# Four output buffers and an uneven deal of the last blocks to three sums, in the expert stage of a gated cross-attention block

## What is computed

```python
topk_p, topk_i = jax.lax.top_k(probs, TOP_K)
topk_p = topk_p / jnp.sum(topk_p, axis=-1, keepdims=True)
gates = gates.at[jnp.arange(T)[:, None], topk_i].add(topk_p)
def r_body(acc, p):
    w1, b1, w2, b2, g = p
    return (acc + g[:, None] * (jnp.maximum(flat @ w1 + b1, 0.0) @ w2 + b2), None)
routed_out, _ = jax.lax.scan(r_body, jnp.zeros_like(flat), (rw1, rb1, rw2, rb2, gates.T))
...
x = x + jnp.tanh(g_ffn[0]) * (shared_out + routed_out)
```

## Time and profile before

| what | us |
|---|---|
| median of three runs | 386.02 |
| the three runs | 383.51 to 388.60 |
| the profiled execution | 387.09 |
| its span in the trace | 385.3 |
| expert stage, first to last scatter issued | 218.7 to 368.3 |
| busy in the whole span: PE, DVE, ACT, POOL | 333.4, 240.6, 214.6, 221.7 |

### The profile page before, as it was taken

How to read it: one execution, slowest core, us unless ns; L and a number is a source line. 1 busy time by engine, 2 the same in 40 slices (tenths; PEclk the granted TensorE clock), 3 DMA queues, 4 the chain that set the end, 5 groups by cost and what they waited for, 6 DMA issues and landing times.

```text
span 385.3 us, 8620 instructions
## 1 busy us (share of the span) xinstructions
PE 333.4 (87%) x2574; PEld 262.3 (68%) x2574; DVE 240.6 (62%) x753; ACT 214.6 (56%) x537; POOL 221.7 (58%) x267
## 2 busy tenths in 40 slices
PE   8889999999899988786772999999999999999800
PEld 5567766666666664564541898999999999999700
DVE  7997788789789888569310355555555545445426
ACT  4795899979878877232130455555555555555400
POOL 8466332103013456757774288888788888787830
PEclk9999999999999999699786899999999999999965
DMA  7799999996004014613233488888888888897688
GB/s 227 208 309 310 308 326 315 320 237 205 4 2 134 19 60 125 204 60 117 101 116 125 128 125 144 137 151 138 139 146 147 142 143 141 138 146 108 76 195 282
DMA packets 63295, 62.20 MB, mean 161 GB/s; under 512 B 6258, under 2 KB 61588, under 8 KB 63252
## 3 DMA queue, kind: packets, MB, share of 16 engines
q1 hardware_dynamic: 48532, 44.60, 40.5%
q0 software_dynamic: 13680, 17.05, 27.4%
q10 hardware_dynamic: 1040, 0.01, 0.2%
HBM read 29.01 MB, written 32.63 MB: 160 GB/s over the span
## 4 chain that ended last, share of the span: by engine, by line
PE 55%; DVE 12%; issue 10%; POOL 9%; DMA 8%; ACT 5%; SPq 0%; POOLq 0%; DVEq 0%
PE psum L1608 14%; PE psum L1590 10%; POOL rows_by_block L502 7%; PE psum L1301 6%; PE psum L1348 5%; DVE nmax L906 5%; DMA sum<-ob,xs 5%; PE psum L1581 4%; PE psum L1599 3%; ACT probs L625 2%; PE psum L1319 2%; PE psum L1196 2%; PE psum L1282 2%; PE psum L1401 2%; POOL sum L546 2%
## 5 line engine op out<-in xcount | busy, mean ns | idle before, releaser
L546 POOL DMA_INDIRECT sum<-ob,xs x79 | 122.4, 1549 | 40.1 <-DVE ob L1166 26.9
L906 DVE TENSOR_REDUCE nmax<-psum 128x2 f32<-128x512 f32 x128 | 80.9, 683 | 13.2 <-PE psum L1301 12.3
L1608 PE MATMUL psum<-w,hT 88*128 (+1 forms) x316 | 81.5, 380 | 0.0
L625 ACT ACTIVATE probs<-psum 128x512 f32<-128x512 f32 x128 | 69.5, 599 | 15.3 <-PE psum L1319 13.8
L1166 DVE TENSOR_SCALAR ob<-psum,gate 128x256 f32<-128x256 f32 x79 | 38.2, 484 | 53.5 <-PE psum L1608 38.1
L755 ACT ACTIVATE hT<-psum,b1b 88x128 f32<-88x128 f32 x158 | 48.8, 357 | 35.6 <-PE psum L1599 34.6
L1590 PE MATMUL psum<-w,xT 128*128 x316 | 61.6, 318 | 0.3 <-ACT xT L746 0.3
L1608 PEld LDWEIGHTS psum<-w,hT 88*128 88x128 f32 (+1 forms) x316 | 53.8, 190 | 4.6 <-issue 0.3
L746 ACT ACTIVATE xT<-psum 128x256 f32<-128x256 f32 x79 | 30.3, 384 | 46.3 <-PE psum L1581 46.2
L502 POOL DMA_INDIRECT rows_by_block<-Vx,slot x48 | 47.6, 991 | 14.4 <-issue 14.1
L425 POOL CAST Qx<-nmax 128x8 fp32r<-128x8 f32 x32 | 6.3, 197 | 74.2 <-DVE nmax L906 74.1
(11 more groups left out here) (194 smaller groups left out, 468.6 us busy)
## 6 DMA issues: line engine op xcount, KB each, us to landing
rows_by_block<-blank SPq DMA_DIRECT2D x1, 10744.0 KB, 38.2
xs<-rows_by_block SPq DMA_DIRECT2D x79, 136.0 KB, 2.9
w<-in_L_ffn_rw_dram SPq DMA_DIRECT2D x2, 2816.0 KB, 22.1
w<-in_L_ffn_rw_dram SPq DMA_DIRECT2D x16, 352.0 KB
sum<-blank SPq DMA_DIRECT2D x3, 1152.0 KB, 13.4
w<-sum SPq DMA_DIRECT2D x12, 256.0 KB, 5.3
sum<-ob,xs POOLq DMA_INDIRECT x79
x_sb<-in_x_dram SPq DMA_DIRECT2D x4, 256.0 KB, 3.9
```

The source lines that it names most:

```text
L546: pool.indirect_dma_start(yd[i], bass.IndirectOffsetOnAxis(ap=xs[b % ROWS_AHEAD][:, X_ID:X_ID + 1].bitcast(U32), axis=0), ob[i][:, :], Non ...
L625: act.activation(probs[g % 2][:, :, n, :], st_bank(g, n)[:, :].rearrange("p (t q) -> p t q", t=TB), ACT.Exp, scale=SCALE).then_inc(exp_ok, 1)
L906: dve.tensor_reduce(nmax[i % 2][:, :, n], S_BANK[(4 * i + n) % SB][:, :].rearrange("p (t k) -> p t k", t=TB), AX.X, ALU.max, negate=True). ...
L1608: ins = pe.matmul(Y_BANK[b % 2][:, 0:D], hT[b % 2][0:rows, c, :], w2[0:rows, bass.ds(expert[b], 1), c, :].rearrange("p a n -> p (a n)"), s ...
```

## The change

There are now four buffers `ob`, used as b mod 4, while there are still three sums. Which sum a block goes to stands in a list: b mod 3 for blocks 0 to 74, and then 0, 1, 0, 1 for blocks 75 to 78, so that sum 2 gets its last scatter from block 74. `added_before(b)` counts the earlier blocks of the same sum, and every wait on `summed` is worked out from it: DVE's wait ahead of writing a buffer is now for block b-4, POOL's for the last block of the same sum (b-3, but b-2 for blocks 77 and 78), SP's for block b-12 as before. The sums are read back and added in the order of their last blocks: 2, 0, 1. A spare piece of SBUF shrinks by the fourth buffer's size, so the later tensors keep their places.

```diff
-    SUMS, ROWS_AHEAD = 3, 12
-    SPARE = 1488
-    assert ROWS_AHEAD % SUMS == 0 and HC < P
+    SUMS, ROWS_AHEAD, OUTS = 3, 12, 4
+    SPARE = 1232
+    assert HC < P
+    sum_of = [b % SUMS for b in range(NB)]
+    sum_of[NB - 4:] = [(NB - 4) % SUMS, (NB - 3) % SUMS] * 2
+    order = sorted(range(SUMS), key=lambda i: max(b for b in range(NB) if sum_of[b] == i))
+    in_sum = [sum_of.count(i) for i in range(SUMS)]
+    def added_before(b):
+        return sum_of[:b].count(sum_of[b])
...
-        ob = [sb(f"ob{i}", [P, D]) for i in range(SUMS)]
+        ob = [sb(f"ob{i}", [P, D]) for i in range(OUTS)]
...
             for n in range(SUMS):
-                i = (NB + n) % SUMS
-                sp.wait_ge(summed[i], 16 * len(range(i, NB, SUMS)))
+                i = order[n]
+                sp.wait_ge(summed[i], 16 * in_sum[i])
...
             for b in range(NB):
-                i = b % SUMS
+                i = sum_of[b]
                 pool.wait_ge(ob_ok, b + 1)
-                if b >= SUMS:
-                    pool.wait_ge(summed[i], 16 * (b // SUMS))
+                if added_before(b):
+                    pool.wait_ge(summed[i], 16 * added_before(b))
                 pool.indirect_dma_start(yd[i], ...
-                                        ob[i][:, :], None, compute_op=ALU.add).then_inc(summed[i], 16)
+                                        ob[b % OUTS][:, :], None, compute_op=ALU.add).then_inc(summed[i], 16)
...
             def block_out(b):
-                i = b % SUMS
                 dve.wait_ge(o_mm, b + 1)
                 dve.wait_ge(gate_ok, b + 1)
-                if b >= SUMS:
-                    dve.wait_ge(summed[i], 16 * (b // SUMS))
-                dve.tensor_scalar(ob[i][:, :], Y_BANK[b % 2][:, 0:D], gate[b % 2][:, 0:1], None, ALU.mult).then_inc(ob_ok, 1)
+                if b >= OUTS:
+                    dve.wait_ge(summed[sum_of[b - OUTS]], 16 * (added_before(b - OUTS) + 1))
+                dve.tensor_scalar(ob[b % OUTS][:, :], Y_BANK[b % 2][:, 0:D], gate[b % 2][:, 0:1], None, ALU.mult).then_inc(ob_ok, 1)
```

More of the change, by code:

```diff
@@ L351, in _ @@
                     sp.wait_ge(xb_mm, b - ROWS_AHEAD + 1)
-                    sp.wait_ge(summed[b % SUMS], 16 * ((b - ROWS_AHEAD) // SUMS + 1))
+                    sp.wait_ge(summed[sum_of[b - ROWS_AHEAD]], 16 * (added_before(b - ROWS_AHEAD) + 1))
                 sp.dma_start(xs[r][:, :], xd[b * P:(b + 1) * P, :]).then_inc(xs_ld[r], 16)
             for n in range(SUMS):
-                i = (NB + n) % SUMS
-                sp.wait_ge(summed[i], 16 * len(range(i, NB, SUMS)))
+                i = order[n]
+                sp.wait_ge(summed[i], 16 * in_sum[i])
                 if n == 0:
```

## The result

The changed kernel is a little slower. Its median over 20 executions is 387.89 us against 385.52 us of the kernel before in the same comparison. The ratio is 1.0055, 95% interval 1.0031 to 1.0079; it isn't that of the two medians, since it leaves out executions more than 1.5% above the fastest of their kernel. Four later comparisons gave smaller ratios, 1.0008 to 1.0047, so the 2.4 us between the medians overstate the loss: over all executions it is 1.2 us. The time forecast was 384.5 us, in a range of 381.0 to 387.8.

The account below looks back on a forecast made before the run. It took the end to be bound by the transfers. Last scatter landing at 374.3 plus 6.0 us to the last load gives 380.3 against 381.8, so 386.0 - 1.5 = 384.5 us; range 381.0 to 387.8.

Parts of the forecast that it names:

- The base: POOL's start of block 76's scatter: four buffers remove its lag behind PE, gaining 0.9 us, bounds 0 and 1.
- Scatter 76 beside four loads: Early read-back of sum 2: four loads beside block 76's scatter, half the excess over 3.9 us, so it takes 5.3 us.
- The hand-over: Between block 76's scatter and block 78's: no term of its own; the quiet 3.9 us reached to the release.
- Scatter 78: Last scatter, beside the four loads of sum 0: 5.3 us, from 369.0 to a landing at 374.3.
- Behind the last scatter: From the last scatter's landing to the last load's: 6.0 us instead of 6.77, bounds 6.0 and 6.8.
- Rival 2: Slower: early loads sit on one sum's chain, scatters 76 and 78 take 6.7 us each; 388.1 us, chance 0.20.
- rule on semaphore writes: A DMA's semaphore write lands only after that engine's earlier writes, so block 76's landing waits for loads queued before it.
- rule on turns between queues: DMA engines alternate between queues by packet, so a scatter beside loads is held up little, landing near 3.9 us.
- Rival 1: The loads don't hinder the scatters at the end: 4.3 us less, 381.7 us, chance 0.20.
- DVE's waits for scatters: Expert stage, sign of being right: these waits fall from 15.3 us to under 3.
- a sign against me, scatter 76 over 6 us: Sign of being wrong: block 76's scatter, forecast at 5.3 us, takes over 6 us, pointing to the slower rival.

Follow-up runs that it names:

- buffers_only: Against the changed kernel: four output buffers kept, but every block b on sum b mod 3 and the old read-back order; ratio to before 1.0026.
- deal_only: Against the changed kernel: three output buffers as before, with the uneven deal and read-back order 2, 0, 1 kept; ratio to before 1.0032, repeated 1.0035.
- hold_reads: Against the changed kernel: even deal, and SP loads nothing before all three sums have landed; four buffers kept; ratio to before 1.0062.
- read_after_77: Against the changed kernel: even deal, and the loads of sum 1 wait for block 77 instead of 76; four buffers kept; ratio to before 0.9997.
- late_read: Against the changed kernel: SP's first load of sum 2 also waits until block 76's scatter has landed; ratio to before 0.9990, repeated 0.9980.

## Why the prediction was wrong

The sign was wrong. The step that failed most is the price of the four early loads on scatter 76, and behind it the hand-over and the base, as follows.

- *The base.* I took POOL's lag at the end (0.93 us) from one profile and counted its removal in full. The changed kernel has no lag: block 76 starts at 366.63 - 367.81 = -1.18 us, exactly as forecast (363.70 - 364.88), and so in all its five traces. But three of five traces of before have next to none, so the gain in this start is 0.4 us on the mean, and buffers_only has a tail of 19.3. Nor does the fourth buffer alone decide it: both traces of deal_only start at -1.18 with three buffers, and hold_reads at -0.70 with four.
- *Scatter 76 beside four loads.* Forecast 5.3 us, half of the excess for half of the loads. Measured 6.2, 5.7, 6.4, 6.8 and 6.2: mean 6.3. Four loads cost about as much as eight had. A scatter whose first load went out 1.7 us or more behind its start took at most 3.9 us in every trace, and before, only the first four were issued sooner: 0.03 to 1.5 us behind block 78's start, the other four from 2.3 us on. I counted eight, and halved a price that belonged to four.
- *The hand-over.* My 5.3 us lie halfway between 3.9, which reaches to the release behind a scatter and holds 0.2 us of hand-over, and 6.70, which ends at the landing and holds none. When POOL has been standing still, the next scatter starts 0.73 us behind the landing (372.81 to 373.54). It comes once on the chain.
- *Scatter 78.* Forecast 5.3; measured 4.9, 5.2, 5.4, 4.5, 6.1: mean 5.2. The number is right, and its reason is not: this scatter too had four loads beside it, issued 0.6 to 0.9 us behind its start where those of scatter 76 began within 0.1 us of it. In deal_only they begin 0.4 us behind it, and it takes 6.4 and 6.5.
- *Behind the last scatter.* Forecast 6.0 us instead of 6.8. Measured 384.25 - 378.43 = 5.8 in the first trace, and 5.2 to 5.8 in the five. Right in kind, and on the mean 0.6 us too long.

Together: -1.18 + 6.3 + 0.7 + 5.2 + 5.2 to 5.8 + 3.5 gives a tail of 19.7 to 20.3; the mean of the five traces is 19.9. The forecast was 18.9. Scatter 76 adds 1.0 us to it and the hand-over 0.7, and the read-back behind the last scatter takes 0.6 away. The forecast stood against a base of 20.4 that should have been 19.6. So a forecast gain of 1.5 us was a loss of 0.3 in the traces' tails.

Rival 2 named the mechanism: two collisions on the chain of one sum. Its price was too high for scatter 78: it has a tail of 22.5 us, where 19.9 were measured. That its 388.1 us nearly meet the first median of 387.89 is chance: it had a loss of 2.1 us, and all executions together have 1.2. The Trainium skill's rule on semaphore writes ("DMA: Bandwidth & Descriptors", section "Queues, rings and completion order") fits what the runs show of loads issued at a scatter's start: 5.7 to 7.2 us with them, 3.75 in hold_reads. No run tells it from other ways in which loads could delay a scatter. The same section's rule on turns between queues, as the prediction read it, would have kept scatter 76 near 3.9, and no run with loads at its start bears that out. Rival 1 is excluded by the same runs.

Right: DVE's waits for scatters vanished, POOL followed PE to block 76, the first loads went out near block 74's landing, and the last two blocks were released by landings. What I had listed as a sign against me, scatter 76 over 6 us, came in four of the five traces.

## What to carry to other kernels

A transfer moved forward into a busy stretch has to be priced on what waits for the transfers beside it: here one megabyte of early loads made a scatter of 3.7 us take 6.3 (means), on a chain that the same change had tightened from three sums to two. Take the base from more than one trace before counting a stall as gain; two of five traces of the same kernel had it. And wherever the twelve loads went out together, they took 12.0 to 13.4 us from the first issue to the last landing, whatever ran beside them. Moving fewer bytes there may shorten the end more than rearranging what they collide with, but no run here tried it.

## What the runs showed that I had not expected

- A scatter beside loads issued at its start takes 5.7 to 7.2 us, one with loads issued 1.9 us behind it 3.6 (read_after_77). When the loads are issued decides, not only that they are under way; whether by their order or by their traffic is open.
- From a landing to the start of the next scatter POOL takes 0.73 us if it stands waiting, against about 0.1 us if the landing comes as it gets there (360.89 to 360.97 and 364.68 to 364.78 in the changed kernel's chain).
- The version that does best is late_read, with a mean of 386.1 us over 22 executions and tails of 18.7 and 19.1. Its ratio, 0.9980 [0.9946, 1.0014] in the larger comparison, does not set it apart from the kernel before.
